# One stream of eight attention stages in a two-kind attention and expert kernel: preparation placed beside units of other stages

## The reference

```python
h = take(W, x)                       # [4, 512, 256]
h = h + local_attention(layernorm(h))   # 16 heads of 16, windows of 128: own window (causal) and the one before; q,k,v,Wo with biases
n = layernorm(h)
h = h + full_attention(n) + moe(n)
# full_attention: 16 heads of 16, all 512 keys, no mask, no output projection
# moe: gate = softmax(n @ W_gate + b); combine = the 2 largest of 8, 0 elsewhere
#      moe = sum_e combine[e] * (n @ W_experts[e] + b_experts[e])
```

## Time and profile before

| | |
|---|---|
| median of 3 runs | 700.95 us (699.73 to 702.8) |
| the profiled execution | 699.81 us, of which its span is 698.1 us |
| PE busy | 621.2 us, 89% |
| DVE busy | 443.3 us, 63% |
| ACT busy | 267.3 us, 38% |
| POOL busy | 88.7 us, 13% |
| mean granted clock of TensorE | 0.951 |

### The profile page before, as it was taken

The page is one execution under the profiler, slowest core; times in us unless marked ns, Lnnn a source line. Parts: engine busy times, 40 slices in busy tenths (PEclk is TensorE's granted clock), DMA queues, the critical chain, the costliest instruction groups (busy, mean ns, idle before and its releaser), DMA issues.

```text
span 698.1 us, 10588 instructions
## 1 busy us (share of the span) xinstructions
PE 621.2 (89%) x4196; PEld 327.2 (47%) x4196; DVE 443.3 (63%) x943; ACT 267.3 (38%) x345; POOL 88.7 (13%) x112
## 2 busy tenths in 40 slices
PE   3956599969999999969999999879999989789996
PEld 2534366524335666434335656334335656344332
DVE  3443365649986655659985755659885713579871
ACT  0301254200477554300567563200666551200675
POOL 3403202500000003400000003400000000200001
PEclk9975799989999999989999999989999999989999
DMA  8285103677100104777000106676000000660000
GB/s 250 82 159 107 46 3 88 135 150 154 18 1 2 34 2 93 140 159 151 2 0 3 33 2 131 128 149 137 1 1 3 32 3 7 128 137 0 1 2 31
DMA packets 26704, 47.24 MB, mean 68 GB/s; under 512 B 4760, under 2 KB 22816, under 8 KB 23584
## 3 DMA queue, kind: packets, MB, share of 16 engines
q1 hardware_dynamic: 25888, 44.48, 29.7%
q0 software_dynamic: 768, 2.10, 1.0%
HBM read 31.62 MB, written 14.68 MB: 66 GB/s over the span
## 4 chain that ended last, share of the span: by engine, by line
PE 64%; DMA 12%; issue 9%; DVE 6%; SPq 3%; ACT 2%; POOL 2%; another core or an unknown queue 1%; POOLq 0%; ACTq 0%
PE OB L880 12%; PE ST L973 10%; PE SC L815 7%; DMA KS<-scratch 6%; PE ST L848 5%; PE SC L821 5%; PE ST L858 4%; PE ST L786 4%; PE SC L823 2%; DMA scratch<-parts 2%; PE ST L860 2%; PE X L889 2%; DVE neg_max L572 2%; SPq L292 2%; PE ST L991 2%
## 5 line engine op out<-in xcount | busy, mean ns | idle before, releaser
L458 ACT ACTIVATE prob<-ST 128x1024 f32<-128x1024 f32 x192 | 183.0, 987 | 151.4 <-PE ST L848 85.1
L572 DVE TENSOR_REDUCE neg_max<-SC 128x1 f32<-128x512 f32 x256 | 172.5, 689 | 52.8 <-PE SC L815 51.3
L973 PE MATMUL ST<-w_exp,xT 128*128 128x512 f32 x256 | 134.3, 624 | 0.0
L815 PE MATMUL SC<-KS,QS 96*128 96x512 bf16 x256 | 99.8, 392 | 27.9 <-DMA KS<-scratch 25.4
L880 PE MATMUL OB<-prob,VS 128*32 128x256 f32 (+1 forms) x1536 | 116.7, 384 | 1.5 <-ACT prob L458 0.9
L434 ACT COPY shiftT<-X 8x512 bf16<-8x512 bf16 x32 | 18.1, 566 | 146.4 <-PE X L830 146.4
L848 PE MATMUL ST<-QS,KS 98*128 98x512 bf16 x256 | 72.8, 379 | 1.2 <-DVE h L691 0.5
L821 PE MATMUL SC<-KS,QS 96*128 96x256 bf16 (+1 forms) x256 | 58.1, 281 | 16.9 <-DVE neg_max L578 7.6
L973 PEld LDWEIGHTS ST<-w_exp,xT 128*128 128x128 f32 x256 | 50.1, 200 | 48.2 <-issue 40.7
L815 PEld LDWEIGHTS SC<-KS,QS 96*128 96x128 bf16 x256 | 24.9, 97 | 100.9 <-issue 66.4
L581 DVE TENSOR_REDUCE neg_max<-SC 128x2 f32<-128x512 f32 x64 | 44.3, 692 | 31.0 <-PE SC L823 30.9
(11 more groups left out here) (106 smaller groups left out, 646.6 us busy)
## 6 DMA issues: line engine op xcount, KB each, us to landing
scratch<-parts SPq DMA_DIRECT2D x96, 128.0 KB
QS<-scratch SPq DMA_DIRECT2D x16, 384.0 KB, 5.2
KS<-scratch SPq DMA_DIRECT2D x16, 384.0 KB, 7.1
QS<-scratch SPq DMA_DIRECT2D x16, 256.0 KB, 7.5
KS<-scratch SPq DMA_DIRECT2D x16, 256.0 KB, 8.4
w_exp<-in_L_ffn_W_experts SPq DMA_DIRECT2D x2, 1024.0 KB
QS<-scratch SPq DMA_DIRECT2D x16, 128.0 KB, 8.8
KS<-scratch SPq DMA_DIRECT2D x16, 128.0 KB, 9.0
```

Of the source, the lines that this page charges most:

```text
L458: act.activation(dst, src, ACT.Exp, scale=SCALE).then_inc(s_prob[kind], 1)
L572: dve.tensor_reduce(neg_max[FULL][:, i, head:head + 1], SC[k % 2][:, :], AX.X, ALU.max, negate=True).then_inc(s_max[kind], 1)
L815: pe.matmul(bank[:, :], QS[FULL][0:SHIFT_ROW, head, i * P:(i + 1) * P], KS[FULL][0:SHIFT_ROW, head, :], start=True, stop=True).then_inc(s_ ...
L973: mm = pe.matmul(ST[:, bank, :], xT[FULL][:, c, t * P:(t + 1) * P], w_exp[:, c, 2 * j:2 * j + 2, :], start=(c == 0), stop=(c == NC - 1))
```

## The change

The work is laid out as one stream of eight stages, `STAGES`: local 0, local 1, local 2, full 0, local 3, full 1, full 2, full 3. A table, `PREPS`, puts the preparation of a later stage into the half slots of an earlier one: normalisation, turning, projections ("local", "full"), the output projection ("out") and the experts ("moe", one job of one expert and two token tiles in each slot). Local 0 and local 1 are both prepared before the first stage. The stage stacks QS and KS alternate; the pieces of the stack of stage s+1 are issued by SP one in a slot of stage s.

Besides: all short-lived PSUM results take turns in two banks R, where a job first waits until the job two before has been read (`claim`); ST has three single banks and ACT takes the exponentials bank by bank; `parts` and `rest` exist once, not once for each kind; the local transposed scores have no mask matmul, POOL sets the masked probabilities to zero (`mask`), and `times_v` comes two slots after its unit in a local stage; the full `times_v` is one matmul of 512 columns for each head, not two of 256; an expert's matmul has 256 columns, not two experts' 512; the copy of the turned x is on ACT; the 31 matmuls that only kept PE busy after the start and in the last middle part are gone, 11 at the start stay; rows of h are updated in place. V is packed with a stride of 20 columns and exists three times.

```diff
-def ahead_of(kind, b, u, more):
...
+STAGES = ((LOCAL, 0), (LOCAL, 1), (LOCAL, 2), (FULL, 0), (LOCAL, 3), (FULL, 1), (FULL, 2), (FULL, 3))
...
+PREPS = {
+    START: (("local", 0, 0), ("local", 1, 13)),
+    0: (("local", 2, 0),),
...
+    3: (("out", 2, 0), ("full", 1, 9), ("moe", 0, 0)),
...
+    7: (),
+}
...
+            def claim(job):
+
+                n = JOB[job]
+                if n >= 2:
+                    name, of, i = JOBS[n - 2]
...
+                    if name == "q":
+                        pe.wait_ge(s_rest, at(of, 4, i + 1))
...
+                    if name == "moe":
+                        pe.wait_ge(s_moe, at(of, NT * E, 2 * i + 2))
+                return bank_of(job)
...
+            def first_part(p, i):
+                kind = STAGES[p][0]
+                act.wait_ge(s_qk_ps, at(p, 4, i + 1))
+                if p > 0:
+                    act.wait_ge(s_written[i // 2], 32 * PARTS * p)
...
+            def mask(s, u):
+
+                pool.wait_ge(s_prob, SCORES_BEFORE[s] + BANKS[LOCAL] * (u + 1))
+                own = prob_local[:, u % 2, u // 2 % 2, :, 0:P]
+                pool.affine_select(out=own, in_=own, compare_op=ALU.is_ge, fill=0.0, base=0,
+                                   pattern=[[0, GH], [1, P]], channel_multiplier=-1).then_inc(s_masked, 1)
...
+            def slot(s, u):
+                kind = STAGES[s][0]
+                rows = rows_beside(s, u)
+                quarters = [rows[i * len(rows) // 4:(i + 1) * len(rows) // 4] for i in range(4)]
+                per = BANKS[kind] // 2
+                for e in range(per):
+                    scores(s, u, e)
+                for step in quarters[0]:
+                    row_scores(*step)
+                half_slot(s, 2 * u, quarters[1])
+                for e in range(per, 2 * per):
+                    scores(s, u, e)
+                for step in quarters[2]:
+                    row_scores(*step)
+                for step in units_times_v(s, u):
+                    times_v(*step)
+                half_slot(s, 2 * u + 1, quarters[3])
```

More of the change, by code:

```diff
@@ L95, in ahead_of @@
     if head < H:
-        return [(kind, b, SMAX_TILES[kind] * head + i) for i in range(SMAX_TILES[kind])]
-    if kind == FULL and more:
-        first, end = (-(-SMAX_TILES[LOCAL] * LEAD[LOCAL] * (head - H + j) // LEAD[FULL]) for j in (0, 1))
-        return [(LOCAL, b + 1, k) for k in range(first, end)]
-    return []
+        return [(s, TILES[kind] * head + i) for i in range(TILES[kind])]
+    if s == LAST:
+        return []
+    after = STAGES[s + 1][0]
+    first, end = (-(-TILES[after] * LEAD[after] * (head - H + j) // LEAD[kind]) for j in (0, 1))
@@ new lines, in rows_beside, with units_times_v, shift_turned @@
+    return [(s + 1, k) for k in range(first, end)]
+def units_times_v(s, u):
+    units = []
+    if u == 0 and s > 0:
+        units.append((s - 1, UNITS - 1))
+    if PV_LAG[STAGES[s][0]] <= u < UNITS:
+        units.append((s, u - PV_LAG[STAGES[s][0]]))
+    return units
+def shift_turned(s, u):
+    kind = STAGES[s][0]
+    if u % 4 == 1 + kind and u < 12:
+        return G * s + u // 4 + 1
+    if s < LAST and u == (13 if kind == LOCAL and STAGES[s + 1][0] == LOCAL else 14):
+        return G * (s + 1)
+    return None
@@ new lines, in half_slot_jobs @@
+def half_slot_jobs(s, t):
+    if s > START and t < 0:
+        s, t = s - 1, HALF_SLOTS + t
+        if s == START:
+            return []
+    jobs = []
+    if s > START:
+        if t % 2 == 1 - STAGES[s][0] and shift_turned(s, t // 2) is not None:
+            jobs.append(("shift", shift_turned(s, t // 2), 0))
+        if t % 2 == 1 and output_turned(s, t // 2) is not None:
+            jobs.append(("o", output_turned(s, t // 2), 0))
+    for what, b, first in PREPS[s]:
+        jobs += prep_jobs(what, b, t - first)
+    return [job for job in jobs if job[0] not in READ_LATER] + [job for job in jobs if job[0] in READ_LATER]
@@ new lines, in prep @@
+            def prep(what, b, step):
+                if what in ("local", "full"):
+                    p = STAGE[(LOCAL, FULL)[what == "full"], b]
+                    if step == Q_STEP[1] + 4:
+                        write_parts(p, 0)
+                    if step == Q_STEP[3] + 4:
+                        write_parts(p, 1)
+            for t in range(HALF_SLOTS):
+                for what, b, first in PREPS[START]:
+                    prep(what, b, t - first)
+                    for m in range(2):
+                        if b == 0 and t - first == Q_STEP[2 * m + 1] + 4:
+                            for piece in range(STACK_PIECES):
+                                stack(0, m, piece // 2, piece % 2, 1)
@@ L331, in _ @@
+            write_out(B - 1)
+            for m in range(2):
+                sp.wait_ge(s_written[m], 32 * PARTS * len(STAGES))
+            sp.wait_ge(s_out, 16 * B)
         @block.gpsimd
@@ L592, in maxima @@
[L592 to L603 removed]
+                    group = G * s + g
@@ new lines, in half_slot @@
+            def half_slot(s, t, rows):
+                for name, of, i in half_slot_jobs(s, t - 1):
+                    if name == "q":
+                        leave_rest(of, i)
+                    if name == "o":
+                        normalise(of)
+                    if name == "moe":
+                        add_expert(of, i)
+                for step in rows:
+                    maxima(*step)
+                for what, b, first in PREPS[s]:
+                    prep(what, b, t - first)
@@ new lines, in expert @@
+            def expert(b, n, between):
+                bank = claim(("moe", b, n))
+                e = n % E
+                for half in range(2):
+                    if half == 1:
+                        between()
+                    t = 2 * (n // E) + half
+                    for c in range(NC):
+                        mm = pe.matmul(bank[:, half * D:(half + 1) * D], xT_full[b % 2][:, c, t * P:(t + 1) * P],
+                                       w_exp[:, c, e, :], start=(c == 0), stop=(c == NC - 1))
+                mm.then_inc(s_moe_ps, 1)
```

1378 lines of the change are left out of this document (689 added, 689 removed).

## The result

The changed kernel takes 681.37 us (median of 4 runs, 674.84 to 685.65) beside 701.14 of the kernel before: 0.969 times, 95% interval 0.962 to 0.976. It is faster by 20 us, where 70 were forecast; 681 lies 9 us above the range. A second set gave 0.974 [0.968, 0.980]. One of the four executions fell in a slower state, and the ratio leaves it out. The profiled execution took 684.10 us, 682.4 of them span.

A forecast was written before the change was run, and what follows sets the result against it. PE was taken to bound most of the kernel. Start 69.4, slots 524, waits 20, slower clock 3, unnamed pause 4 and 8 behind the stream gave 628 us of span, 631 us in all; range 604 to 672.

The forecast's parts named there:

- Waits between the two: Handshake waits between PE and DVE in the stream: 4%, 20 us, with ends of 0 and 6% (31 us).
- the larger of the two gives 524 us: Stream length from taking the larger of PE and DVE time in each of 128 slots; PE alone gives 500 us.
- 551: The eight stages together: 524 us of slots with the waits, slower clock and unnamed pause added.
- the third rival: PE waits at nearly each `claim`: 224 jobs at 0.35 us add 78 us, giving 709 us; chance 0.05.
- pauses that end on DVE at job boundaries: Sign that the forecast is wrong: PE's pauses end on DVE or ACT at job boundaries.
- 3 for the slower clock: At the head of stage 0, a slower PE clock adds 3 us.
- 6.5 us of a range of 0 to 12.5: At the start, local 1's twelve writes before the first shift rows in one queue delay the first transposed scores.
- The pause of 8 us: Unnamed loss at 70 us in the kernel before; 4 us of it counted, ends 0 and 8.
- no PE wait for stack pieces in the stream: Sign of being right: no PE pause for stack DMAs after the first stage; the 6 us holes are gone.
- the product with V of 512 columns takes 1.00 us: Price of the full product with V; 1.7 us instead would be a sign of being wrong, costing 45 us.
- the second rival: POOL's masks hold DVE, 19 us in each local stage on DVE: 631 + 38 = 669 us; chance 0.07.
- The first, late shift rows: Rival: shift rows arrive late in local stages, 28 groups by 1.4 us each: 631 + 39 = 670 us; chance 0.18.

The follow-up runs named there:

- Edits of order and banks alone: Changed kernel plus the late turn, shift rows sent first, three banks R with two ST, the spread and the writes last: 637.63 us, 0.911 times the kernel before.
- the late turn: Changed kernel, but in full stages the shift is turned in the second half of its slot, not the first: 669.74 us, 0.952 times the kernel before.
- the third bank: Changed kernel with three banks R and two ST; a job waits for the job three before: 665.98 us, 0.963 times the kernel before.
- the run with the shift first: Changed kernel, but SP sends group 0's shift rows ahead of local 1's twelve writes: 676.02 us, 0.976 times the kernel before.
- the spread: Statistics and normalisation one tile per half slot, not two: 680.44 us on the changed kernel; 645.89 with late turn, shift first and three banks too.
- the half maxima: Late turn, shift first, three banks and the spread, with each row maximum over half its columns: 633.50 us, 0.904 times the kernel before.
- the writes last: Late turn, shift first, three banks and the spread, with six writes of local 2 sent behind stage 1's shift rows in stage 0: 637.63 us, 0.911.

## Why the prediction was wrong

**The step that failed** is "Waits between the two. [...] I take 4%, 20 us", and under it "taking for each of the 128 slots the larger of the two gives 524 us". The larger of two sums is a slot's time only if each engine may run ahead of the other by as much as a slot needs. Within a slot they are tied: the turn needs the last maxima, the job behind it needs a bank that DVE frees only after them. Measured, the stream took 49 us more than 551. Edits of order and banks alone took 38 of these back: 12 in stages 0 to 2 (a part of them by the clock), 10 in stage 3, 5 in stage 4 and 11 in stages 5 to 7. By edit, the late turn gave back about 8, nearly all in stage 6; the third bank 5 to 6 in stages 3 and 4 each and, less the 3.9 that it costs in stage 7, 4 in stages 5 to 7. I had the neighbour rows for it, 29.3 us of waits at two banks, and used them for the third rival only. That rival's sign was right; 0.35 us for each of 224 jobs was too much. The waits at claims are some 17 us, 0.08 for each job; all waits at jobs of R, 45 us, would be 0.20, and most of these are for a job's own input, which the third rival left out. It had named pauses that end on DVE at job boundaries as a sign of being wrong, and they came.

**"3 for the slower clock"** was sized at the head of stage 0 alone. I had read that the slow clock came with stack transfers and took it as gone with them. The clocks of stages 0 to 4 in the changed kernel (0.88, 0.85, 0.97, 0.97, 0.98) leave out about 22 us of full clock, an estimate from the windows: each stage's length times what its clock lacks to 1. It is the most that the clock can have cost, and 6 us of it are in stage 0. What one stage can lose by it is measured: the same list took 57.5 to 66.7 us in stage 1. Twice the lower clock went with a thin PE, at DVE's pile in stage 1 and at the stop for shift rows; that the first causes it is not shown, since one execution had the pile and kept its clock.

**The start.** The writes of local 1 between the high stack and the first shift rows: I took 6.5 us of a range of 0 to 12.5, and they cost 4.4, as the run with the shift first shows. What the sum had too small is the preparation of local 1 ahead of DVE's first maxima. The prediction saw it, put it at about 50 us and took it as running beside the DMA queue, at no cost; only 1.7 us for one projection stand in the sum. DVE's first maximum came at 59.58 us, 13.3 us later than before. With the writes out of the way the first transposed scores still come at 69.7, 8.6 us later than in the kernel before, though the shift rows land in 2.10 us there and took 5.72 before. The pause of 8 us is absent from the changed kernel's chain, so 4 us of the sum were too much in it; a pause of that kind, of 2.0 to 5.0 us at 70 to 72 us, is back in four profiled executions of the faster kernels, and its cause stays open.

**Right**: no PE wait for stack pieces in the stream; the product with V of 512 columns takes 1.00 us; experts 0.87 a half job; exponentials 0.595 us and nearly hidden (6.7 us of waits of PE's weight loads in stage 7); masks 0.637 us (forecast 0.6 to 1.2), hidden; 7.5 us behind the stream. POOL blocked DVE only where an instruction lay wholly in SBUF, the maxima kept to 0.69 us, and the second rival did not come true. The first, late shift rows, came true in the small: 1.0 us in the stream of the changed kernel; where the spread brought six writes ahead of them it was 5 at one place.

**Where the rest lies.** Without these losses the same stream takes 637.63, 7 us above the forecast. Its stages are 38 us longer than the larger sums of 524 (160.4 for 144 in stages 0 to 2, 228.3 for 212 in stages 5 to 7), of which 27 were in the forecast as waits, slow clock and pause, and the start is 3 us earlier. Of stages 0 to 2 the half maxima gave back 8, but from 166.5 us, with the stop for the shift rows still in them; with the writes last they were not run. Of the 16 in stages 5 to 7 the two ST banks cost 3.9, in stage 7. What the rest is, PE's own time by instruction or more of DVE's, no run here tells.

## What to carry to other kernels

When two engines are folded into common slots, don't price a slot by the larger sum: follow one slot in order, and for each shared bank ask which instruction frees it and what stands ahead of that. An instruction that needs the other engine's latest result belongs at the slot's end. A third bank for jobs was worth more here than a third one for scores (15 us net alone, 7 beside the late turn), at a price of 3.9 us in the stage that has no jobs to share it. Small transfers that someone waits for go to the queue before large ones that nobody waits for.

## What was not expected of the hardware

- The granted clock fell to 0.50 in the middle of the stream, after 5 us in which PE worked 2.96 us, and stayed there for 13.7 us of nearly full PE (144.4 to 158.1). In another execution PE worked 2.94 of 5 us at the same place and kept 1.00. The same instructions took 57.5, 61.6 and 66.7 us in stage 1 of three executions, at 1.00, 0.92 and 0.85.
- DVE's normalisation from SBUF to SBUF took 0.72 us beside POOL's mask and up to 1.236 beside POOL's subtraction, in place of 0.406, and a shift row of 0.175 us took 1.07. Each slow normalisation ended 0.14 to 0.15 us after a POOL instruction. DVE's rest (one PSUM and one SBUF input) kept to 741 to 753 ns.
- Two small transfers behind six writes and two stack pieces in SP's list took 5 us to land, PE stood for them, and the clock was at 0.50 for 6.8 us around the end of the stop (122.4 to 129.2).
- More columns on PE left stages 0 to 2 no longer in two kernels out of two, with the clock higher, and took 4.2 us for 3.4 us of columns in a stage where PE had no gap.
